# Tile h2's columns by block transposes on VectorE and a DRAM scratch; b tables on GpSimd; VectorE's order within a tile rewritten

## The reference

```python
dt_Lambda = dt[:, None, 0] * Lambda[None, :, 0] + 1j * (dt[:, None, 1] * Lambda[None, :, 1])
Wc = Wc * num * _reciprocal(den * Lam, EPS)
K = jnp.einsum('chn,hnl->chl', Wc, jnp.exp(P))          # P = dt_Lambda * pos; real part taken
h = K.real
h = h + einsum('bsk,nk->bsn', _layernorm(h), weight * block_mask)
x2 = _layernorm(h)
weights = sparsemax(x2 @ W_router.T + b_router)
h = h + x2 @ W_base.T + b_base + einsum('bser,bse,ero->bso', x2 @ lora_A, weights, lora_B)
```

## Time and profile before

| | |
|---|---|
| median of 3 runs | 535.89 us (535.52 to 536.78) |
| profiled execution, its own time | 535.71 us |
| its span | 533.9 us |
| PE busy | 486.2 us, 91% |
| PE weight load busy | 407.1 us, 76% |
| DVE busy | 411.5 us, 77% |
| ACT busy | 255.9 us, 48% |
| POOL busy | 125.7 us, 24% |
| mean granted clock of TensorE | 0.983 |

### The profile page before, as it was taken

How to read it: one execution, slowest core, us unless ns; L and a number is a source line. 1 busy time by engine, 2 the same in 40 slices (tenths; PEclk the granted TensorE clock), 3 DMA queues, 4 the chain that set the end, 5 groups by cost and what they waited for, 6 DMA issues and landing times.

```text
span 533.9 us, 7434 instructions
## 1 busy us (share of the span) xinstructions
PE 486.2 (91%) x2467; PEld 407.1 (76%) x2467; DVE 411.5 (77%) x866; ACT 255.9 (48%) x469; POOL 125.7 (24%) x110
## 2 busy tenths in 40 slices
PE   3257978889899999999999999999999999999995
PEld 2155757778687888888887888787888888888884
DVE  7989866898787987888787878788988878764241
ACT  3763385947263554646463626263644546323200
POOL 0577952630020303030303020020303030303020
PEclk9996989989999999999999999999999999999999
DMA  8994013021212121221203031212121211212011
GB/s 298 400 294 101 1 46 118 1 83 45 79 47 79 44 79 44 61 62 39 83 19 88 17 88 35 79 44 79 44 79 46 79 41 41 79 35 84 1 39 39
DMA packets 28763, 40.82 MB, mean 76 GB/s; under 512 B 10760, under 2 KB 21192, under 8 KB 28744
## 3 DMA queue, kind: packets, MB, share of 16 engines
q1 hardware_dynamic: 28368, 40.49, 25.1%
q10 hardware_dynamic: 376, 0.10, 0.1%
HBM read 23.80 MB, written 16.78 MB: 76 GB/s over the span
## 4 chain that ended last, share of the span: by engine, by line
PE 36%; DVE 35%; issue 17%; ACT 9%; POOL 1%; DVEq 1%; DMA 0%; ACTq 0%; POOLq 0%
PE acc_b L455 15%; PE acc_a L455 13%; DVE b_sb L1127 4%; PE turnp L448 2%; DVE tmp L1093 2%; DVE tmp L1112 2%; PE turnp L439 2%; DVE x_lo L1174 2%; ACT x_hi L715 2%; ACT x_hi L680 2%; DVE b_sb L1111 2%; PE small L479 1%; DVE st L1135 1%; PE acc_b L420 1%; DVE wa_raw L1015 1%
## 5 line engine op out<-in xcount | busy, mean ns | idle before, releaser
L917 POOL TENSOR_TENSOR h<-h,st 128x1024 f32<-128x1024 f32 x16 | 30.3, 1894 | 337.7 <-PE turnp L448 337.7
L455 PE MATMUL acc_a<-wa_hi,x_hi 128*128 128x512 f32 x256 | 84.1, 405 | 0.5 <-DVE h L1145 0.5
L455 PE MATMUL acc_b<-wb_hi,x_hi 128*128 128x512 f32 x256 | 84.5, 406 | 0.0
L455 PE MATMUL acc_a<-wa_lo,x_hi 128*128 128x512 f32 x256 | 81.6, 395 | 0.0
L455 PE MATMUL acc_b<-wb_lo,x_hi 128*128 128x512 f32 x256 | 81.3, 394 | 0.0
L455 PE MATMUL acc_a<-wa_hi,x_lo 128*128 128x512 f32 x256 | 81.2, 393 | 0.0
L455 PE MATMUL acc_b<-wb_hi,x_lo 128*128 128x512 f32 x256 | 80.9, 392 | 0.0
L455 PEld LDWEIGHTS acc_a<-wa_hi,x_lo 128*128 128x128 f32 x256 | 48.8, 190 | 10.6
L455 PEld LDWEIGHTS acc_b<-wb_hi,x_lo 128*128 128x128 f32 x256 | 48.5, 189 | 10.6
L455 PEld LDWEIGHTS acc_b<-wb_lo,x_hi 128*128 128x128 f32 x256 | 48.5, 189 | 10.5
L455 PEld LDWEIGHTS acc_a<-wa_lo,x_hi 128*128 128x128 f32 x256 | 48.8, 191 | 10.1
(11 more groups left out here) (201 smaller groups left out, 913.9 us busy)
## 6 DMA issues: line engine op xcount, KB each, us to landing
h<-rows_out SPq DMA_DIRECT2D x16, 512.0 KB, 3.2
out<-h SPq DMA_DIRECT2D x15, 512.0 KB
rows_out<-b_sb SPq DMA_DIRECT2D x56, 128.0 KB, 2.3
mask_raw<-in_L_attn_mask SPq DMA_DIRECT2D x8, 512.0 KB, 9.8
wa_raw<-in_L_attn_weight SPq DMA_DIRECT2D x8, 512.0 KB, 10.5
wb_raw<-in_L_ffn_W_base SPq DMA_DIRECT2D x8, 512.0 KB, 14.7
rows_out<-tmp SPq DMA_DIRECT2D x8, 128.0 KB, 2.3
xn<-in_x SPq DMA_DIRECT2D x15, 64.0 KB
```

The costliest lines, as they stand in the source:

```text
L455: return pe.matmul(cols, a, rows, start=first, stop=last)
L917: pool.tensor_tensor(h2[par][:, :], h2[par][:, :], st2[:, par, 1:2].to_broadcast([P, L]), ALU.subtract)\
```

## The change

- `h2_transposes` is gone from PE. In its place `h2_turn(t)` (DVE) transposes 32 by 32 blocks of `h2` from SBUF into `b_sb`'s memory, `h2_columns_write` (SP, four DMAs) writes them to a second DRAM scratch and `h2_columns_read` (SP, one DMA) reads them into `x2_raw`, the memory of `x2_lo`. A column's eight chunks now lie interleaved: `h2_high` and `h2_low` read every eighth element, `h2_low` writes every eighth, and PE loads the weights for `x_lo` with that stride of 32 bytes. `h2_low` has both inputs in SBUF, where it had one in PSUM.
- `table_b` of tiles 3 to 15 is POOL's. Its second product goes into `tmp`, which is also where `k_turn` of all tiles now writes.
- DVE's step is in another order: `phases(t + 2)` first, `h2_low(t - 1)` before `attention_residual(t)`, `gates(t - 1)` before `k_turn(t + 1)`, `decay_b` a step earlier, `gated_low` before `table_v`, whose scratch is PSUM (`turnp`) for all tiles. On PE `gated_transpose` stands one chunk earlier. On ACT `x_rows_twice` comes first and `h2_high` after `k_deviation`.
- The reciprocal of the deviation has three operations on DVE where it had five, and one more on ACT.

```diff
             def step(t, par):
-                pe.wait_ge(kt_turned, t + 1)
-                h2_transposes(t - 1, 1 - par)
                 pe.wait_ge(kt_lo, t + 1)
                 for k in range(KC):
                     attention(t, k)
-                pe.wait_ge(h2t_lo, t)
                 if real(t + 1):
                     k_transposed(t + 1)
+                pe.wait_ge(h2t_lo, t)
                 pe.wait_ge(hwt_lo, t - 1)
                 lora_router(t - 1)
...
+            def h2_turn(t, par):
+
+                dve.wait_ge(h2_centred, t + 1)
+                dve.wait_ge(kt_ready, 2 if at(t, 0) else t + 2 if real(t + 1) else TILES)
+                dve.transpose(h2_turned_sb.rearrange("p (q r k) -> p q k r", q=Q, k=KC),
+                              h2[par][:, :].rearrange("p (k q f) -> p q k f", k=KC, q=Q)).then_inc(h2_turned, 1)
...
             def h2_low(t):
                 dve.wait_ge(h2t_hi, t + 1)
-                hi, lo = x2_of(t)
-                dve.tensor_tensor(lo[:, :, :].rearrange("p k n -> p (k n)"), turnp[:, :],
-                                  hi[:, :, :].bitcast(F).rearrange("p k n -> p (k n)"), ALU.subtract)\
-                    .then_inc(h2t_lo, 1)
+                hi, lo, raw = x2_of(t)
+                dve.tensor_tensor(turned_chunks(lo), raw[:, :].rearrange("p (n k) -> p k n", k=KC),
+                                  hi[:, :, :].bitcast(F), ALU.subtract).then_inc(h2t_lo, 1)
...
             def step(t, par):
                 if real(t + 3):
                     load_x(t + 3)
+                h2_columns_write(t)
                 if real(t + 1):
-                    k_rows(t + 1)
+                    k_rows_write(t + 1)
+                    k_rows_read(t + 1)
+                h2_columns_read(t)
                 sp.wait_ge(out_ready, t)
                 store(t - 1, 1 - par)
...
             def table_b(t):
 
+                if later(t, 1):
+                    pool.wait_ge(kt_ready, t)
+                if later(t, 2):
+                    pool.wait_ge(h2_out, (t - 1) * OUT)
+                pool.wait_ge(v_chain, t * V_STEPS + 3)
                 pool.wait_ge(b_chain, t * 3 + 1)
...
             def step(t, par):
                 add_bias(t - 1, 1 - par)
+                if real(t + 2):
+                    table_b(t + 2)
 
             pool.wait_ge(bias_in, 16)
             add_bias(0, 0)
+            table_b(3)
             steps(pool, step)
```

More of the change, by code:

```diff
@@ L231, in by_pair @@
             return v[:, :, :].rearrange("p a (g x) -> p g a x", g=G)
-        def turned_of(t):
-            return tmp[:, :] if not later(t, 2) else flat(b_sb)
+        k_turned, h2_turned_sb = tmp[:, :], flat(b_sb)
         h_n = lambda v, n: v.rearrange("p (h n) -> p h n", n=n)
@@ L341, in _ @@
             load_x(3)
-            k_rows(2)
+            k_rows_write(2)
+            h2_columns_write(1)
+            k_rows_read(2)
+            h2_columns_read(1)
             load_x(4)
@@ L475, in lora_router @@
             def lora_router(t):
-                x_hi, x_lo = x2_of(t)
                 for k in range(KC):
-                    pe.matmul(small[:, 0:2 * CAT], x_hi[:, k, :], wr[:, k, :, :].rearrange("p s n -> p (s n)"),
+                    x_hi, x_lo = x2_chunks(t, k)
+                    pe.matmul(small[:, 0:2 * CAT], x_hi, wr[:, k, :, :].rearrange("p s n -> p (s n)"),
                               start=k == 0, stop=False)
-                    mm = pe.matmul(small[:, 0:CAT], x_lo[:, k, :], wr[:, k, 0, :], start=False, stop=k == KC - 1)
+                    mm = pe.matmul(small[:, 0:CAT], x_lo, wr[:, k, 0, :], start=False, stop=k == KC - 1)
                 mm.then_inc(cat_ready, 1)
@@ L489, in base @@
             def base(t, k, halves=(0, 1)):
-                x_hi, x_lo = x2_of(t)
-                product(acc_b, x_hi[:, k, :], x_lo[:, k, :], wb_hi, wb_lo, k, k == 0, False, halves)
+                x_hi, x_lo = x2_chunks(t, k)
+                product(acc_b, x_hi, x_lo, wb_hi, wb_lo, k, k == 0, False, halves)
             def experts(halves=(0, 1)):
@@ L914, in add_bias @@
             def add_bias(t, par):
-                pool.wait_ge(h2t_ready, t + 1)
                 pool.wait_ge(h2_dev, t + 1)
+                pool.wait_ge(h2_turned, t + 1)
+                if later(t, 1) and real(t + 1):
+                    pool.wait_ge(attn_ready, t + 2)
                 pool.tensor_tensor(h2[par][:, :], h2[par][:, :], st2[:, par, 1:2].to_broadcast([P, L]), ALU.subtract)\
@@ L1080, in u @@
                     return u12[:, i].unsqueeze(3).to_broadcast([P, HT, NA, C])
-                second = v_second if not later(t, 2) else tmp[:, :].rearrange("p (h a c) -> p h a c", h=HT, a=NA)
                 dve.wait_ge(w_ready, t + 1)
@@ L1195, in step @@
             def step(t, par):
+                if real(t + 2):
+                    phases(t + 2)
+                h1_reciprocal(t)
                 h2_low(t - 1)
+                dve.wait_ge(out_stored[par], t * 8 - 8 * par)
+                attention_residual(t, par)
                 h2_reciprocal(t - 1, 1 - par)
                 if real(t + 1):
-                    table_b(t + 1)
-                h1_reciprocal(t)
-                if real(t + 2):
-                    phases(t + 2)
-                dve.wait_ge(out_stored[par], t * 8 - 8 * par)
-                attention_residual(t, par)
+                    k_low(t + 1)
+                h2_turn(t, par)
+                gates(t - 1, 1 - par)
                 if real(t + 1):
-                    k_low(t + 1)
                     k_turn(t + 1)
-                gates(t - 1, 1 - par)
                 if real(t + 2):
                     v_factors(t + 2)
+                    decay_b(t + 2)
+                gated_low(t - 1)
+                if real(t + 2):
                     table_v(t + 2)
-                gated_low(t - 1)
                 if at(t, TILES - 1):
@@ L1275, in _ @@
             wb_lows(8)
+            h2_turn(0, 0)
             reciprocal_of_norm(1)
@@ L1297, in _ @@
             k_turn(2)
+            h2_turn(1, 1)
             v_factors(3)
+            decay_b(3)
             table_v(3)
```

149 lines of the change are left out of this document (80 added, 69 removed).

## The result

| | before | after |
|---|---|---|
| median | 536.32 us (4 runs beside it) | 547.9 us (547.13 to 548.27, 4 runs) |
| ratio | | 1.0216, 95% interval 1.0201 to 1.0232 |
| span of the profiled execution | 533.9 us | 545.3 us |
| step between attention(3) and attention(14) | 28.52 us | 28.49 us |

The change makes the kernel 11.6 us slower; forecast were 527.8 us and a range of 519 to 534.5.

The account below looks back on a forecast made before the run. PE's own sum was taken to bound the loop. Terms +5.4 (first step), -11 x 1.10, -0.8 (step without x transposes) and -0.6 (end) gave -8.1: span 533.9 to 525.8, median about 527.8 us, range 519 to 534.5.

Parts of the forecast that it names:

- PE's steps of 27.42: Loop steps on PE: without eight transposes (0.79) and the wait (0.31), 28.52 falls to 27.42, -1.10 each.
- (b): Unknown price of PE's strided weight loads: at most 0.12 each, judged from wa_raw's seven in 0.86; nothing taken.
- The rival: PE's strided x_lo loads cost double, uncovered in lora_router: 0.9 a step, +12.6, 540.4 us; chance 0.06.
- (a): Unknown price of 32-byte strides in h2_high, h2_low and h2_turn: none taken, upper end 1.0 each, about +4.
- (c): Unknown price of h2_turn reading SBUF rather than PSUM: 1.2 to 2.2 us, hidden in the loop.
- The hand-over at the first step: First loop step: POOL's table_b(3) and add_bias(1) stretch DVE's phases(4), PE waits 6.5 for h2_low(1); attention(3) +5.4.
- The slow clock: After PE's 6.5 wait in the first loop step its clock halves, adding 1.7 us.
- the lock: Shared SBUF port: a DVE operation with both inputs in SBUF waits out POOL's running one; without it, 7.8 less.
- first rival: Clean hand-over at the first loop step: PE waits under 1, attention(3) at 143.3, 7.8 earlier, 520 us; chance 0.22.
- The part ahead of the loop: Before the loop: gates(0) 0.8 later eats the 0.79 of transposes, attention(2) stays at 115.2, no loss.
- The end: After attention(15): tile 15's columns go through DRAM, costing PE 0.2 against 0.79 of transposes saved: -0.6.

## Why the prediction was wrong

- **PE's steps of 27.42: wrong, by the stride.** The failing step is "(b) PE's weight load with the stride", of which the prediction says "I take nothing". It costs 1.24 a step where only the stride was added, and 28.49 - 27.23 = 1.26 where only it was taken away (the two versions that land in `tmp`, in their first steps). The rest of the term held and was a little better than said: no wait ahead of experts, and 27.23 for 27.42 where the stride was gone and the columns had a place of their own. With the place that the change gives them (`x_lo`'s own memory) and no stride no kernel was run. Over the twelve steps from attention(3) the stride is 12 x 1.24 = 14.9, less 12 x 0.19: 12.6 of the 19.5 us between forecast and result. The rival named it at 0.9 for lora_router and left out base's 0.31, which I called covered; it had a chance of 0.06.
- **Why 0.06.** I read wa_raw's seven strided loads in 0.86 as full rate. They are loads for transposes of f32, not fp32r products, and the mean duration by form, which no row of mine has, differs between the strided ones and those of `wb_raw`, contiguous transposes beside them. Kernel before:

```profile
L399 PEld LDWEIGHTS acc_b<-kst,wa_raw 128*128 128x128 f32 x64 | 11.6, 219 | 8.5 <-issue 4.2 <-ACT wa_raw L628 4.1
L420 PEld LDWEIGHTS acc_b<-kst,wb_raw 128*128 128x128 f32 x64 | 7.5, 141 | 8.1 <-issue 4.1 <-ACT wb_hi L643 3.0
```

  219 ns strided, 141 contiguous. Why their spacing of 0.12 doesn't show it was not tried. The 78 ns more would have made (b) doubtful; its size on fp32r loads, 130 ns, stood in no row of the kernel before.
- **(a), stride on DVE and ACT: no penalty taken, 1.1 and 1.0 measured** (`h2_high` 2.14 against 1.03, `h2_low` 2.25 against 1.22). The upper bound of 1.0 each was nearly right; `h2_turn` took 2.20, the top of (c)'s 1.2 to 2.2; the loop hides all three, as said.
- **The hand-over at the first step: the chain came as told, the size of the step by luck.** GpSimd started at 122.8 (forecast 119.4), `phases(4)` ended at 134.8 (132.6), the wait was 6.16 (6.5), the granted clock 0.50 behind it. attention(3) was 8.4 late, not 5.4: 2.95 came from the part ahead and 5.45 from the step. The step took 35.97, the forecast gives it 151.1 - 115.2 = 35.9, but two errors of about 1 us cancel in that. The slow clock cost some 0.8, not 1.7 (lora_router and base took 15.26, up to experts at 152.70, against 14.50 in the later step above), and the stride added the 1.23 that was not in the sum. Nor was the lock all of it: ScalarE's path, late for x and slowed by the stride, ended at 133.21, only 2.1 ahead of `h2_low(1)`, so on this trace the lock can account for at most 2.1 of the 6.16 by itself. The prediction has this path in its first rival, ending at 128.2.
- **The part ahead of the loop: no loss forecast, 2.95 measured.** Gates put 0.8 later, "so attention(2) starts at 115.2 as before", failed: gates(0) began 1.6 later (104.23 against 102.63), and three of their operations were held by GpSimd (1.55, 1.88 and 2.30) where two were before (1.28 and 2.13), besides the strided loads of lora_router(0). With `add_bias(0)` behind the gates attention(2) is early, 114.31, with those strided loads still in it.
- **The end: -0.6 forecast, +3.04 measured.** Tile 15 goes through DRAM with strided `h2_high`, `h2_low` and loads. The trace after divides it: the end holds lora_router and base of two tiles, 2 x 1.23 = 2.46 for the stride; TensorE waits 1.32 for gates(14), two operations of which take 1.56 and 2.16 where the loop has 0.23 and 0.22; the transposes take off 0.79; together 2.99. The wait for `h2_low(15)`, 0.2 in the forecast, did not come: the slower loads and the wait for the gates cover it. Contiguous, through DRAM, the end is 47.9, with waits of 0.97 for the gates and 0.78 for `h2_low(15)`; with TensorE's transposes for tiles 0, 1 and 15 it is 46.5, before's value.
- **Misses together,** forecast -8.1 against +11.4 of span: attention(3) 3.0, the twelve steps 12.9 (the 12.6 above, and 0.3 of the last one), the end 3.6.

## What to carry to other kernels

Before a layout is made strided, price each of its readers by the mean of its own kind of instruction (type, width, what covers it), not by the spacing of another kind; where there is no row of that kind, as here, the price is open and belongs in the range with a chance well over 0.06. 24 loads a step that take 0.13 us more each added 1.24 us, 4% of a loop that is TensorE's sum. A round trip through DRAM suited the steady state here, where there was time for it (27.23 a step for 28.13); where the pipeline fills and drains, TensorE's own transpose was better (a first step of 29.29 for 37.21), and the two can stand side by side. In a queue, what is needed at once goes ahead of what is stored.

## What was unexpected of the hardware

- A weight load of 128 fp32r columns takes 190 ns contiguous, 198 at a stride of 8 bytes, 309 at 16, 317 to 323 at 32. VectorE writing 1024 elements has the same cliff: 1.22, 1.22, 2.03, 2.18 us.
- Under matmuls of 512 columns a load with a stride of 32 bytes costs 0.31 / 16 = 0.02 us each, under the router's 272 and 136 columns 0.92 / 8 = 0.115.
- A read of 512 KB issued 0.75 us behind a store of 512 KB landed after 8.6 us, ahead of it after 3.3.
